# A two-layer kernel of scans, attention and experts: the first side input is loaded alone, its products move to VectorE and PSUM, and the V projections stand right behind the scores

## The chip, the cores and the metric

The kernel runs on one core of a Trainium2 chip. The metric is the device time of one execution in microseconds, which is to be small. Its engines each run their own instruction stream in order and meet at semaphores: TensorE (PE in the profile), VectorE (DVE), ScalarE (ACT), GpSimd (POOL) and SyncE (SP, whose queue issues nearly all transfers here).

## The reference

Inputs are x and a side input f, both 4 x 256 x 256 (batch B, positions T, channels C). Three parts follow one another:

```python
# cond: two decaying sums over the positions, forward and backward, per channel
ek, ekv = exp(min(f, 30)), exp(min(f, 30)) * f
a_t = a_{t-1} * decay + ekv_t          # and b_t with ek_t, in both directions
euk = exp(min(u + f, 30))
y = sigmoid(x) * (nf + nb - ekv + euk * f) / max(df + db - ek + euk, 1e-8) * (0.8 + 0.2 * tf)
# attention over y: 16 heads of 128, causal, softmax
x = x + W_O @ softmax(mask(K(y) Q(y)) / sqrt(128)) V(y)
# a second cond with its own w, u on the new x gives y2; 8 experts, the best 2 weigh in
x = x + sum_e gates[e] * (y2 @ expert_w[e] + expert_b[e])
```

## The kernel before, in words

All products are float32 in three passes: each operand is held as a high part (`_hi`, rounded by ScalarE from PSUM) and a low part (`_lo`, the rest, subtracted by VectorE or GpSimd), and `three` (L847) issues high x high, high x low and low x high. A result in PSUM thus becomes an operand in two steps, a ScalarE copy and then a VectorE subtraction: `qk_high`/`qk_low`, `v_high`/`v_low`, `pT_high`/`pT_low`, `z_high`/`z_low`. Weights get the same split by `refill`, on ScalarE (`w_hi`, L356) and then on GpSimd (`w_lo`, L266).

The attention is 16 blocks (four batches by four groups of four heads) of four units each, one head of one batch to a unit, so 64 units; u is the unit, i = u // 4 its block and h = u % 4. Every engine has a loop `for u in range(UNITS)`, written by hand so that the loops mesh. In unit u TensorE does `scores(u)`, `project_qk(u + 2)`, `values(u - 2)`, `turn(u - 1)` (the transposes of the probabilities), and then in the units with h = 0 or 1 one half of the V projection, `project_v(i, h)`, in those with h = 2 or 3 one half of `output` of the block before. VectorE starts a unit with `v_low` of the V half of the unit before, then `maxima(u)`, `reciprocals(u)`, `qk_low(u + 2)`, `z_low(u - 2)`, `pT_low(u - 1)`. ScalarE does `exps(u)`, `qk_high(u + 2)`, `z_high(u - 2)`, `pT_high(u - 1)`, and `v_high` last. GpSimd multiplies the probabilities by the reciprocals (`shares`, L298) after its other work of the unit. `values(4 i)` stands in unit 4 i + 2 and needs both V halves of block i as high and low parts (`v_ready`).

The conds of the next batches and of the second layer are cut into pieces, which tables (`DVE_PLACES`, `ACT_PLACES`, `POOL_PLACES`) put into the units: "M" behind the maxima or exponentials, "E" at the end of the unit. Eight conds in all; the first, of batch 0, is written out ahead of the loops, since nothing can start without its y. It works by channel half c: `min`, exponentials, forward scans into `f_xd` and `f_xn`, scaling on ScalarE, backward scans, then two long reciprocals and `first_y(c)`. While it runs, TensorE does `WARM` pairs of products whose result nobody reads (L1012).

SP issues the loads in one list: temb, f of batch 0 (`in_f0`), the Q and K weights of group 0, x of batch 0, and so on. Behind the loop come the experts on TensorE (`experts(j)`, 32 of them, with `logits`, `gates_turn` and `base` of the four batches between them) and `add_experts(j)` on VectorE; `acc` goes out in eight stores.

## Time and profile before

| | |
|---|---|
| time, median of 3 runs | 388.52 us (388.48 to 388.64) |
| the profiled execution's own time | 388.69 us |
| its span, first to last instruction | 386.8 us |
| TensorE busy | 357.1 us (92%), 2534 instructions |
| VectorE busy | 315.2 us (81%) |
| ScalarE busy | 219.7 us (57%) |
| GpSimd busy | 210.1 us (54%) |
| mean granted clock of TensorE | 0.994 |

Busy times are sums over the span; ends of matmuls are modelled. The time of a run is 1.9 us above the span in the profiled execution. Times in the rows are microseconds from the span's start; a releaser behind an arrow is what ended the idle time before an instruction.

### The profile page before, as it was taken

To read this page: it belongs to the slowest core of one execution; us is meant where nothing else is said; L and a number is where in the kernel's file an instruction comes from. 1 tells how busy PE (TensorE), PEld (TensorE's weight loads), DVE (VectorE), ACT (ScalarE), POOL (GpSimd) and SP (SyncE) were. 2 spreads that over 40 slices of the span, in tenths; PEclk is the share of its full clock that TensorE was granted. 3 is DMA by queue.
4 is the path that set the end of the run, shared out by engine and by line. 5 is a ranking of instruction groups with operands and counts; after the bars stand their busy time and mean duration, and the time that the engine had idled before them with its cause. 6 is when DMAs were issued, how large, how long until landed. Compare 5 with 4: busy or idle time off the path is not lost.

```text
span 386.8 us, 7608 instructions
## 1 busy us (share of the span) xinstructions
PE 357.1 (92%) x2534; PEld 332.8 (86%) x2534; DVE 315.2 (81%) x883; ACT 219.7 (57%) x616; POOL 210.1 (54%) x231
## 2 busy tenths in 40 slices
PE   0578888999999999999999999999999998999996
PEld 0467878999999899999999999999999987877885
...
DMA packets 4598, 14.14 MB, mean 37 GB/s; under 512 B 840, under 2 KB 1872, under 8 KB 3920
## 3 DMA queue, kind: packets, MB, share of 16 engines
q1 hardware_dynamic: 4416, 13.65, 10.6%
...
q10 hardware_dynamic: 144, 0.00, 0.0%
...
## 4 chain that ended last, share of the span: by engine, by line
PE 81%; DVE 10%; issue 2%; POOL 2%; ACT 2%; DMA 1%; SPq 0%; DVEq 0%; ACTq 0%; POOLq 0%
PE psQK L850 9%; PE psQK L852 9%; PE psQK L851 9%; PE psT L910 5%; PE psZ L850 4%; PE psO L852 4%; PE psO L850 4%; PE psO L851 4%; PE psS L901 4%; PE psS L850 4%; PE psZ L852 4%; PE psZ L851 4%; PE psS L851 4%; PE psS L852 4%; PE psV L850 4%; PE psV L852 3%
## 5 line engine op out<-in xcount | busy, mean ns | idle before, releaser
L472 ACT ACTIVATE prob<-prob,ntop 128x256 f32<-128x256 f32 (+1 forms) x128 | 57.3, 449 | 93.3 <-DVE ntop L690 93.3
L301 POOL TENSOR_SCALAR prob<-prob,rsum 128x128 f32<-128x128 f32 x64 | 38.9, 607 | 104.7 <-DVE rsum L698 104.7
L850 PE MATMUL psQK<-y_hi,w_hi 128*128 128x256 f32 x256 | 73.3, 286 | 1.3 <-DVE y_lo L613 1.1
L852 PE MATMUL psQK<-y_hi,w_lo 128*128 128x256 f32 x256 | 73.0, 285 | 0.0
L851 PE MATMUL psQK<-y_lo,w_hi 128*128 128x256 f32 x256 | 72.9, 285 | 0.0
L302 POOL TENSOR_SCALAR prob<-prob,rsum 128x256 f32<-128x256 f32 x64 | 59.8, 935 | 0.0
L266 POOL TENSOR_TENSOR w_lo<-raw,w_hi 128x512 fp32r<-128x512 f32 x40 | 52.9, 1334 | 6.6 <-ACT w_hi L356 6.4
L850 PEld LDWEIGHTS psQK<-y_hi,w_hi 128*128 128x128 f32 x256 | 49.3, 193 | 2.2 <-DVE y_lo L613 1.3
L852 PEld LDWEIGHTS psQK<-y_hi,w_lo 128*128 128x128 f32 x256 | 49.3, 193 | 0.0
L851 PEld LDWEIGHTS psQK<-y_lo,w_hi 128*128 128x128 f32 x256 | 49.3, 193 | 0.0
L702 DVE TENSOR_TENSOR qk<-psQK,qk 128x512 fp32r<-128x512 f32 x64 | 43.6, 682 | 6.5 <-ACT qk L460 4.8
L850 PE MATMUL psZ<-pT,v_hi 128*128 128x256 f32 x128 | 37.0, 289 | 9.0 <-issue 4.6
L850 PE MATMUL psO<-z_hi,w_hi 128*128 128x256 f32 x128 | 38.6, 302 | 0.0
L460 ACT ACTIVATE qk<-psQK 128x512 fp32r<-128x512 f32 x64 | 36.9, 577 | 0.6 <-PE psQK L852 0.5
L706 DVE TENSOR_TENSOR v_lo<-psV,v_hi 128x512 fp32r<-128x512 f32 x32 | 22.0, 689 | 17.9 <-ACT v_hi L466 17.8
L852 PE MATMUL psZ<-pT,v_lo 128*128 128x256 f32 x128 | 36.1, 282 | 0.0
L851 PE MATMUL psZ<-pT,v_hi 128*128 128x256 f32 x128 | 36.1, 282 | 0.0
L852 PE MATMUL psO<-z_hi,w_lo 128*128 128x256 f32 x128 | 36.1, 282 | 0.0
L851 PE MATMUL psO<-z_lo,w_hi 128*128 128x256 f32 x128 | 36.0, 281 | 0.0
L711 DVE TENSOR_TENSOR pT<-psT,pT 128x384 fp32r<-128x384 f32 x64 | 35.0, 547 | 0.5 <-ACT pT L480 0.5
L850 PEld LDWEIGHTS psZ<-pT,v_hi 128*128 128x128 f32 x128 | 24.3, 190 | 11.2 <-issue 8.9
L910 PE MATMUL psT<-identf,prob 128*128 128x128 f32 x192 | 31.3, 271 | 0.0
...
## 6 DMA issues: line engine op xcount, KB each, us to landing
...
out<-fT SPq DMA_DIRECT2D x8, 128.0 KB, 2.0
...
xT<-in_xT SPq DMA_DIRECT2D x1, 512.0 KB, 10.9
wu<-in_wu ACTq DMA_DIRECT2D x1, 4.0 KB, 1.6
```

The source lines that it names most:

```text
L266: pool.tensor_tensor(w_view(w_lo[:, g % 2], kind, part), w_view(raw, kind, part), w_view(w_hi[:, g % 2], kind, part).bitcast(F32), ALU.sub ...
L301: pool.tensor_scalar(prob[:, k, 0:P], prob[:, k, 0:P], rsum[:, k, 0:1], None, ALU.mult)
L302: pool.tensor_scalar(prob[:, k, P:3 * P], prob[:, k, P:3 * P], rsum[:, k, 1:2], None, ALU.mult).then_inc(shared, 1)
L460: act.activation(qk_hi[:, u % 2], psQK[u % 2][:], ACT.Copy).then_inc(qk_hi_done, 1)
L472: ins = act.activation(prob[:, k, lo:hi], prob[:, k, lo:hi], ACT.Exp, scale=-1.0, bias=ntop[:, k, q:q + 1], accum_out=ssum[:, k, q:q + 1])
L702: dve.tensor_tensor(qk_lo[:, u % 2], psQK[u % 2][:], qk_hi[:, u % 2].bitcast(F32), ALU.subtract).then_inc(qk_ready, 1)
L706: dve.tensor_tensor(v_lo[:, i % 2, t], psV[:], v_hi[:, i % 2, t].bitcast(F32), ALU.subtract).then_inc(v_ready, 1)
L711: dve.tensor_tensor(pT[:, k, 1, P:4 * P], psT[:, 0:3 * P], pT[:, k, 0, P:4 * P].bitcast(F32), ALU.subtract).then_inc(pT_ready, 1)
L850: pe.matmul(out, ah, bh, start=first and k == 0, stop=False)
L851: pe.matmul(out, ah, bl, start=False, stop=False)
L852: ins = pe.matmul(out, al, bh, start=False, stop=last and k == n - 1)
L910: ins = pe.transpose(psT[:, n * P:(n + 1) * P], prob[:, u % 2, c * P:(c + 1) * P], identf[:])
```

## The change

It does five things. SP loads f of batch 0 first and waits until it has landed before it issues the next load; temb goes to ScalarE's queue. In the first cond the products `f_ekv` and `f_eukv` and the clamp of `euk` are no longer GpSimd's but VectorE's, and they stand in PSUM banks (`psQK[1]`, `psT`); ScalarE writes the exponentials once, into PSUM, and `WARM` is 5 instead of 7. V halves are projected right behind the scores of their unit (the first one ahead of all scores), copied right behind the exponentials on ScalarE and subtracted behind the reciprocals of the same unit on VectorE. The shares of units 2 and 3 are ScalarE's. `min` and `exps` of the later conds start a unit earlier, and some weight copies of groups 2 to 4 stand at "M". In the end `gates_copy(0)`, `gates_turn(1)`, `pT_high` of the last unit, `y2_last(3)`, `logits(3)`, `gates_turn(3)` and `base(3)` change their places by one step.

```diff
-DVE_PLACES = {"min": (-2, "E"), "xd": (0, "M"), "xn": (1, "M"), "gd": (2, "M"), "gn": (3, "M"), "den": (4, "M"),
+DVE_PLACES = {"min": (-3, "E"), "xd": (0, "M"), "xn": (1, "M"), "gd": (2, "M"), "gn": (3, "M"), "den": (4, "M"),
...
-ACT_PLACES = {"exps": (-1, "E"), "sxd": (0, "E"), "sxn": (1, "E"), "e1": (2, "E"), "yhi": (7, "E")}
+ACT_PLACES = {"exps": (-2, "E"), "sxd": (0, "E"), "sxn": (1, "E"), "e1": (2, "E"), "yhi": (7, "E")}
...
+SHARES_ACT = (2, 3)
 GATE_STEPS = 14
-WARM = 7
+WARM = 5
...
-    f_ek, f_euk = halves(psQK[0]), halves(psS[0])
+    f_ek, f_ekv, f_euk, f_eukv = (halves(bank) for bank in (psQK[0], psQK[1], psS[0], psT))
     f_xd, f_xn = [psV[:, 0:T], psS[1][:, 0:T]], [psZ[:, 0:T], psO[:, 0:T]]
     t0 = tiles[:, 0]
-    f_e1, f_eukv = t0[:, XD], t0[:, XN]
+    f_e1 = t0[:, XD]
...
-        sp.dma_start(temb[:], ap["temb"]).then_inc(in_temb, 16)
+
         load_f(0, 1, in_f0)
+        sp.wait_ge(in_f0, 16)
         load_qk(0)
...
-
-        pool.wait_ge(f_act, 2)
-        pool.tensor_tensor(t0[:, EKV], t0[:, EK], cols(fT, 0), ALU.mult).then_inc(f_pool, 1)
-        pool.wait_ge(f_act, 4)
-        pool.tensor_scalar(t0[:, EUK], t0[:, EUK], EXP_LIMIT, None, ALU.min).then_inc(f_pool, 1)
-        pool.wait_ge(f_pool, 2)
-        pool.tensor_tensor(f_eukv, t0[:, EUK], cols(fT, 0), ALU.mult).then_inc(f_pool, 1)
...
-            shares(u)
+            if u not in SHARES_ACT:
+                shares(u)
...
+        act.dma_start(temb[:], ap["temb"]).then_inc(in_temb, 16)
         act.dma_start(wu[:], ap["wu"]).then_inc(in_wu, 16)
...
-        act.activation(t0[:, EK], t0[:, EK], ACT.Exp).then_inc(f_act, 1)
-        for c in range(CB):
-            act.activation(t0[:, EUK, c], fT[:, 0, c], ACT.Exp, bias=wu[:, 1, c:c + 1]).then_inc(f_act, 1)
+        for c in range(CB):
+            act.activation(f_euk[:, c], fT[:, 0, c], ACT.Exp, bias=wu[:, 1, c:c + 1]).then_inc(f_act, 1)
...
+        def shares(u):
+            k = u % 2
+            act.wait_ge(recipd, u + 1)
+            act.activation(prob[:, k, 0:P], prob[:, k, 0:P], ACT.Copy, scale=rsum[:, k, 0:1])
+            act.activation(prob[:, k, P:3 * P], prob[:, k, P:3 * P], ACT.Copy, scale=rsum[:, k, 1:2]).then_inc(shared, 1)
...
             for kind, part, u in places:
-                at(u, "E", refill, kind, g, part)
+                at(u, "M" if u % GH < TT and g > 1 else "E", refill, kind, g, part)
...
         at(62, "E", gate_exp, 1)
-        at(63, "M", gates_copy, 0)
+        at(62, "E", gates_copy, 0)
         at(63, "E", gates_copy, 1)
...
         qk_high(0)
         qk_high(1)
+        v_high(0, 0)
         cond(1)["exps"]()
         for u in range(UNITS):
+            i, h = u // GH, u % GH
             exps(u)
+            if h < TT and u:
+                v_high(i, h)
             do(u, "M")
             if u + 2 < UNITS:
                 qk_high(u + 2)
             if 2 <= u:
                 z_high(u - 2)
+            if u in SHARES_ACT:
+                shares(u)
             if 1 <= u:
                 pT_high(u - 1)
             do(u, "E")
-            i, h = u // GH, u % GH
-            if h < TT:
-                v_high(i, h)
         z_high(UNITS - 2)
+        pT_high(UNITS - 1)
         tanh(2)
-        pT_high(UNITS - 1)
...
         for c in range(CB):
             forward(f_xd[c], f_ek[:, c], 0, c, 0).then_inc(f_dve, 1)
+        dve.tensor_tensor(f_ekv, f_ek, cols(fT, 0), ALU.mult).then_inc(f_dve, 1)
         for c in range(CB):
             dve.tensor_scalar(decay[:, 1, c], tdec[:], ew[:, 1, c:c + 1], None, ALU.mult).then_inc(pre_dve, 1)
...
+        dve.wait_ge(f_dve, 4)
+        for c in range(CB):
+            forward(f_xn[c], f_ekv[:, c], 0, c, 0).then_inc(f_dve, 1)
+        for c in range(CB):
+            dve.wait_ge(f_act, 4 + c)
+            backward(t0[:, GD, c], f_xd[c], 0, c, 0).then_inc(f_dve, 1)
+        dve.wait_ge(f_act, 3)
+        dve.scalar_tensor_tensor(f_eukv, f_euk, EXP_LIMIT, cols(fT, 0), ALU.min, ALU.mult).then_inc(f_dve, 1)
+        for c in range(CB):
+            dve.wait_ge(f_act, 6 + c)
+            backward(t0[:, GN, c], f_xn[c], 0, c, 0).then_inc(f_dve, 1)
...
             dve.scalar_tensor_tensor(f_xd[c], f_xd[c], 1e-8, f_e1[:, c], ALU.max, ALU.mult).then_inc(f_dve, 1)
 
         def first_y(c):
             dve.tensor_tensor(f_xn[c], f_eukv[:, c], t0[:, GN, c], ALU.add).then_inc(f_dve, 1)
-            dve.wait_ge(f_dve, 15 + 4 * c)
...
         for u in range(UNITS):
-            if 1 <= u:
-                i, h = (u - 1) // GH, (u - 1) % GH
-                if h < TT:
-                    v_low(i, h)
             maxima(u)
             do(u, "M")
             reciprocals(u)
+            i, h = u // GH, u % GH
+            if h < TT:
+                v_low(i, h)
...
         gate_first(2)
         add_experts(5)
+        y2_last(3)
         gate_last(2)
-        y2_last(3)
         add_experts(6)
         add_experts(7)
+        add_experts(8)
         gate_first(3)
-        add_experts(8)
+        add_experts(9)
         gate_last(3)
-        for j in range(9, 8 * B):
+        for j in range(10, 8 * B):
             add_experts(j)
...
-        pe.wait_ge(f_dve, 6)
+        pe.wait_ge(f_dve, 7)
         for n in range(WARM):
             for c in range(CB):
-                pe.matmul(psQK[1][:, c * T:(c + 1) * T], identf[:], fT[:, 0, c], start=True, stop=True)
+                pe.matmul(psQK[0][:, c * T:(c + 1) * T], identf[:], fT[:, 0, c], start=True, stop=True)
 
         pe.wait_ge(wlo_qk, 2)
-        pe.wait_ge(f_dve, 18)
+        pe.wait_ge(f_dve, 20)
         project_qk_half(0, 0)
         project_qk_half(1, 0)
         y_waits(0)
         project_qk_half(0, 1).then_inc(qk_done, 1)
         project_qk_half(1, 1).then_inc(qk_done, 1)
+        project_v(0, 0)
         for u in range(UNITS):
             i, h = u // GH, u % GH
             scores(u)
+            if h < TT and u:
+                project_v(i, h)
             if u == UNITS - 2:
                 logits(1)
             if u + 2 < UNITS:
@@ -1029,11 +1038,7 @@
                 values(u - 2)
             if u:
                 turn(u - 1)
-            if u == UNITS - 1:
-                gates_turn(1)
-            if h < TT:
-                project_v(i, h)
-            elif i:
+            if h >= TT and i:
                 output(i - 1, h - TT)
             if u == UNITS - 6:
                 logits(0)
@@ -1041,6 +1046,7 @@
                 experts(0)
                 gates_turn(0)
             if u == UNITS - 1:
+                gates_turn(1)
                 base(0)
                 experts(1)
         experts(2)
@@ -1054,7 +1060,7 @@
             output(len(BLOCKS) - 1, c)
         logits(2)
         base(1)
-        late = {7: [(logits, 3)], 9: [(gates_turn, 2)], 10: [(base, 2)], 11: [(gates_turn, 3)], 12: [(base, 3)]}
+        late = {8: [(logits, 3)], 9: [(gates_turn, 2)], 10: [(base, 2)], 12: [(gates_turn, 3)], 13: [(base, 3)]}
         for j in range(6, 8 * B):
```

VectorE in the first cond before, from the first forward scans on (psV and psS are `f_xd`, psZ and psO are `f_xn`; tiles is the SBUF work space):

```order
L569 SCALAR_TENSOR_TENSOR psV<-decay,psQK 128x256
L569 SCALAR_TENSOR_TENSOR psS<-decay,psQK 128x256
L580 TENSOR_SCALAR decay<-tdec,ew 128x4 x2
L583 TENSOR_SCALAR rest<-decay 128x16
L585 SCALAR_TENSOR_TENSOR rest<-decay,rest 128x16
L586 TENSOR_SCALAR tout<-tf 128x4
L588 TENSOR_SCALAR thalf<-tout 128x4
L569 SCALAR_TENSOR_TENSOR psZ<-decay,tiles 128x256
L569 SCALAR_TENSOR_TENSOR psO<-decay,tiles 128x256
```

And the same place in the change:

```order
L573 SCALAR_TENSOR_TENSOR psV<-decay,psQK 128x256
L573 SCALAR_TENSOR_TENSOR psS<-decay,psQK 128x256
L583 TENSOR_TENSOR psQK<-psQK,fT 128x512
L585 TENSOR_SCALAR decay<-tdec,ew 128x4 x2
L588 TENSOR_SCALAR rest<-decay 128x16
L590 SCALAR_TENSOR_TENSOR rest<-decay,rest 128x16
L573 SCALAR_TENSOR_TENSOR psZ<-decay,psQK 128x256
L573 SCALAR_TENSOR_TENSOR psO<-decay,psQK 128x256
```

The product `f_ekv` is a VectorE instruction now (L583), tout and thalf come later, and both scans of `f_xn` read PSUM (psQK) instead of tiles.

VectorE at the end of unit 1 before, from its scans `gd` to the maxima of unit 2:

```order
L572 SCALAR_TENSOR_TENSOR tiles<-decay,tiles 128x256 x2
L698 RECIPROCAL rsum<-ssum 128x2
L702 TENSOR_TENSOR qk<-psQK,qk 128x512
L711 TENSOR_TENSOR pT<-psT,pT 128x384
L572 SCALAR_TENSOR_TENSOR tiles<-decay,tiles 128x256 x2
L706 TENSOR_TENSOR v_lo<-psV,v_hi 128x512
L689 TENSOR_TENSOR first_mask<-psS,negmask 128x128
```

In the change:

```order
L576 SCALAR_TENSOR_TENSOR tiles<-decay,tiles 128x256 x2
L705 RECIPROCAL rsum<-ssum 128x2
L713 TENSOR_TENSOR v_lo<-psV,v_hi 128x512
L709 TENSOR_TENSOR qk<-psQK,qk 128x512
L718 TENSOR_TENSOR pT<-psT,pT 128x384
L576 SCALAR_TENSOR_TENSOR tiles<-decay,tiles 128x256 x2
L696 TENSOR_TENSOR first_mask<-psS,negmask 128x128
```

`v_lo` moved from the place behind the second pair of scans to the place behind the reciprocals, ahead of `qk` and `pT`.

TensorE before, from the transposes of unit 0 on through the second V half to the scores of unit 2:

```order
L910 MATMUL psT<-identf,prob 128x128 x3
L850 MATMUL psV<-w_hi,y_hi 128x512
L851 MATMUL psV<-w_lo,y_hi 128x512
L852 MATMUL psV<-w_hi,y_lo 128x512
L850 MATMUL psV<-w_hi,y_hi 128x512
L851 MATMUL psV<-w_lo,y_hi 128x512
L852 MATMUL psV<-w_hi,y_lo 128x512
L901 MATMUL psS<-qk 128x256 x2
```

In the change, from the scores of unit 1 on to the first product of the next Q and K:

```order
L907 MATMUL psS<-qk 128x256 x2
L856 MATMUL psS<-qk 128x256
L857 MATMUL psS<-qk 128x256
L858 MATMUL psS<-qk 128x256
L856 MATMUL psV<-w_hi,y_hi 128x512
L857 MATMUL psV<-w_lo,y_hi 128x512
L858 MATMUL psV<-w_hi,y_lo 128x512
L856 MATMUL psV<-w_hi,y_hi 128x512
L857 MATMUL psV<-w_lo,y_hi 128x512
L858 MATMUL psV<-w_hi,y_lo 128x512
L856 MATMUL psQK<-y_hi,w_hi 128x256
```

The six products of the V half stand behind the scores (psS) and ahead of twelve products of psQK, which they used to follow, with the transposes.

## Rows read from the trace of the kernel before

**Rows 1.** Waits of TensorE: us in total, times, longest.
```profile
PE psQK L1012 <- DVE tiles L572: 10.3, 1, 10.3
PE psZ L850 <- issue: 4.6, 7, 1.5
PE psZ L850 <- DVE v_lo L706: 3.0, 1, 3.0
...
PE psZ L850 <- DVE pT L711: 1.5, 3, 1.0
PE psV L964 <- ACT tiles L454: 1.1, 1, 1.1
PE psQK L850 <- DVE y_lo L613: 1.1, 1, 1.1
...
PE psV L950 <- DVE y L681: 0.7, 1, 0.7
```

**Rows 2.** The chain that ended last: start, us, what.
```profile
1.32 4.88 DMA fT<-in_fT
...
59.34 1.53 issue
...
97.04 0.48 issue
...
243.67 0.46 issue
...
316.55 0.72 issue
```

**Rows 3.** Timeline of the start, VectorE's, GpSimd's and TensorE's instructions: start, us.
```profile
6.23 0.43 DVE L554 TENSOR_SCALAR tiles<-fT 128x512 f32<-128x512 f32 x1 [6.23 <-DMA fT<-in_fT]
...
8.76 0.58 DVE L580 TENSOR_SCALAR decay<-tdec,ew 128x4 f32<-128x4 f32 x2
...
11.24 1.69 DVE L569 TENSOR_TENSOR_SCAN psO<-decay,tiles 128x256 f32<-128x256 f32 x1
...
12.85 0.66 DVE L572 TENSOR_TENSOR_SCAN tiles<-decay,psV 128x256 f32<-128x256 f32 x1
...
13.65 8.06 PE L1012 MATMUL psQK<-fT,identf 128*128 128x256 f32 x28 [10.35 <-DVE tiles L572]
...
15.21 7.61 POOL L266 TENSOR_TENSOR w_lo<-raw,w_hi 128x512 fp32r<-128x512 f32 x6 [2.84 <-ACT w_hi L356]
15.47 0.42 DVE L600 SCALAR_TENSOR_TENSOR psS<-psS,tiles 128x256 f32<-128x256 f32 x1
...
18.13 1.11 DVE L607 TENSOR_TENSOR psZ<-tiles 128x256 f32<-128x256 f32 x1
...
21.62 1.50 DVE L607 TENSOR_TENSOR psO<-tiles 128x256 f32<-128x256 f32 x1
...
24.57 0.39 PE L850 MATMUL psQK<-y_hi,w_hi 128*128 128x256 f32 x1 [1.06 <-DVE y_lo L613]
```

**Rows 4.** DMA issues of the page: KB each, median us to landing.
```profile
out<-fT SPq DMA_DIRECT2D x8, 128.0 KB, 2.0
```

**Rows 5.** Time to landing of the three loads of xT, by tile.
```profile
DMA to landing us min/median/max: 7.2/9.6/10.9
```

**Rows 6.** Windows: length, busy PE, PEld, DVE, ACT, POOL (instructions), clock, DMA share, GB/s.
```profile
40.00:50.00 10.00, 8.98 (x60) 8.64 (x61) 10.00 (x25) 5.79 (x18) 9.12 (x10) 0.83 0.13 37
50.00:60.00 10.00, 8.65 (x58) 7.53 (x56) 7.64 (x19) 8.42 (x23) 7.69 (x9) 1.00 0.36 121
...
42.00:43.00 1.00, 1.00 (x6) 1.00 (x6) 1.00 (x5) 1.00 (x4) 0.78 (x2) 0.50 0.00 0
```

**Rows 7.** Timeline around 96 us, unit 13 going into 14.
```profile
95.73 0.55 DVE L711 TENSOR_TENSOR pT<-psT,pT 128x384 fp32r<-128x384 f32 x1
...
96.72 0.69 DVE L706 TENSOR_TENSOR v_lo<-psV,v_hi 128x512 fp32r<-128x512 f32 x1 [0.44 <-ACT v_hi L466]
```

**Rows 8.** Waits of VectorE: us in total, times, longest.
```profile
DVE v_lo L706 <- ACT v_hi L466: 17.8, 28, 1.6
```

More of the change, by code:

```diff
@@ L585, in _ @@
         dve.scalar_tensor_tensor(rest[:], decay[:], 1.0, rest[:], ALU.add, ALU.mult).then_inc(pre_dve, 1)
+        dve.wait_ge(f_dve, 4)
[9 more added lines that the diff above has]
+            backward(t0[:, GN, c], f_xn[c], 0, c, 0).then_inc(f_dve, 1)
         dve.tensor_scalar(tout[:], tf[:], 0.2, 0.8, ALU.mult, ALU.add).then_inc(pre_dve, 1)
+        for c in range(CB):
+            dve.wait_ge(f_dve, 7 + c)
+            dve.scalar_tensor_tensor(f_xd[c], f_euk[:, c], EXP_LIMIT, t0[:, GD, c], ALU.min, ALU.add).then_inc(f_dve, 1)
         dve.wait_ge(pre_dve, 10)
         dve.tensor_scalar(thalf[:], tout[:], 0.5, None, ALU.mult).then_inc(pre_dve, 1)
[L589 removed]
+        dve.wait_ge(f_act, 9)
         for c in range(CB):
[L591 to L603 removed]
+            dve.wait_ge(f_dve, 12 + c)
             dve.scalar_tensor_tensor(f_xd[c], f_xd[c], 1e-8, f_e1[:, c], ALU.max, ALU.mult).then_inc(f_dve, 1)
@@ L622, in clamp @@
                 if n == 2:
-                    dve.wait_ge(f_dve, 21)
+                    dve.wait_ge(f_dve, 23)
                 if n > 2:
@@ L861, in y_waits @@
             if b == 0:
-                pe.wait_ge(f_dve, 21)
+                pe.wait_ge(f_dve, 23)
             else:
```

31 lines of the change are left out of this document (8 added, 23 removed).

## The prediction

> **What bounds the kernel now.** I read the waits of TensorE first, since it is busy for 92% of the span. They are few: 10.3 us once, in the start, until VectorE's first backward scan releases the idle warm-up products, and then a handful that add up to about 13 us in the other 360 [rows 1]. So the kernel has two parts that can be shortened: the chain from the first load to the first real product, in which TensorE does nothing useful, and single holes later. The chain that ended last says where those are: an "issue" of 0.48 us at 97.04 comes again with every second block, five times up to the one at 243.67 (0.46), and single ones of 1.53 at 59.34 and 0.72 at 316.55 [rows 2]. Each stands ahead of `values`. The timeline around 96 us shows what "issue" hides: `v_lo` ends at 97.41 and the product starts at 97.52, while the other operand, `pT`, had ended at 96.28 [rows 7]. So the second V half is what comes last.
>
> The timeline of the start gives the other part: VectorE starts at 6.23, when f has landed, and the second half of y reaches TensorE at 24.57 [rows 3]. The windows show a third thing: from 40 to 50 us VectorE is busy for 10.00 of 10 us and TensorE's granted clock has a mean of 0.83; at 42 to 43 it is 0.50, the lower of its two levels (1.2 GHz), after TensorE had waited 3.0 us for `v_lo` [rows 1, 6]. A mean of 0.83 over 10 us is 1.7 us of clock lost.
>
> **The start, -5.2 us.** Three terms.
>
> Landing. The load of f is issued at 1.32 and takes 4.88 us, with a megabyte of weights and more behind it on the same queue [rows 2]. Alone, it is issued at about 0.7, where temb was, and 256 KB should take more than the 2.0 us of a store of 128 KB [rows 4] and at most the 4.88. I take 2.8, nearer to the store, since with nothing beside it the queue holds only this load: VectorE starts at 3.5 instead of 6.2, -2.7 us. Bounds: 2.7 (-3.5) and 5.6 (-0.6). What waits behind: the Q and K weights go out 1.6 us later than before, x of batch 0 at about 4.0. x took 7.2 us, the smallest of its three loads [rows 5]; so it lands at 11.2 and its two ScalarE passes, some 0.6 us each, end near 12.5, just when VectorE comes to the step that needs them. temb on ScalarE's queue delays the tiny loads by half a microsecond, which the wait for f covers.
>
> VectorE's chain up to the first backward scan. From the second pair of decays at 8.76 to that scan at 12.85 it takes 4.09 us [rows 3]. The two forward scans of `f_xn` in it lie beside GpSimd instructions; the second takes 1.69 us, where a scan whose data is in PSUM takes 0.66 [rows 3]. With the GpSimd work gone, scans start every 0.6 us and the small instructions every 0.2: decays 0.35, the two of rest 0.4, two scans 1.2, that is 2.0 us. Added are `f_ekv`, about 0.62 (the same shape from PSUM and SBUF is `v_lo`, 0.69 with 0.07 of overlap [rows 7]), as much for `f_eukv` later, and tout and thalf, 0.3, which only moved. 4.09 against 3.54: -0.55 us. Bounds 0 and -1.2.
>
> The two sums of `first_y`. They take 1.11 and 1.50 us, both operands in SBUF, while GpSimd is in its row of six weight subtractions; the instruction of the same size at 15.47, one operand in PSUM, takes 0.42 beside the same GpSimd work [rows 3]. In the change `f_eukv` stands in PSUM, so both should take 0.4: -0.7 and -1.1, together -1.9 us (bounds 0 and -1.9).
>
> So TensorE's second half of y is ready at 24.57 - 5.15 = 19.4. The first V half, now right behind those products, needs six weight pieces from GpSimd, done at 22.8 before [rows 3]; they start when ScalarE gets to them, at about 12.5 instead of 14.5, so they end near 20.7, and V is asked for at 20.8. Nothing to spare, but no loss.
>
> **Units 0 to 7, -2.6 us.** TensorE's waits here are the 3.0, about 1.2 of the 1.5 for `pT`, the 1.53, and 1.7 of clock [rows 1, 2, 6]. The 3.0 us goes: `v_low` of the second half is done in unit 1. But VectorE has no idle time up to 50 us [rows 6] and the same work to do; one instruction more stands there, `min` a unit earlier (0.5), and the first scores start 0.45 later behind the V half. So `pT_low`, the next in line, is waited for in place of `v_lo`, in two or three pieces of 0.5 to 1.4 us, and unit 4 begins on VectorE some 0.6 us late. The wait of 3.0 in one piece, and with it the drop of the clock, should go. What is won comes behind unit 4: in the window from 50 to 60 VectorE has 2.4 us of idle time [rows 6], in which it waits for `v_hi` on ScalarE, and TensorE then for VectorE. In the new order `v_hi` comes right behind the exponentials, and VectorE can use these 2.4 us. With the 1.53 and the rest of `pT` I take -2.6. Bounds: 0 (all given back) and the sum of what is lost, -7. The shares of units 2 and 3 on ScalarE take two GpSimd instructions of about 1.5 us off the way to the transposes; GpSimd is busy for 9.12 of 10 us there [rows 6], so this mainly lets the weights of group 1 keep up with a V half that is asked for 4 us sooner. I count it at nothing.
>
> **Units 8 to 61, -2.3 us.** Five holes of 0.48 [rows 2]. What the holes wait for now is done a unit ahead. Next in line is `pT_low`. It must be ready when `values` comes; between `turn` and `values` TensorE used to do a V half, the scores and Q and K, now in a unit with h = 1 only the last two, some 2.0 us. In the stretch of rows 7 `pT_lo` stands at 95.73 to 96.28 and would be asked for at 97.04, 0.76 us of slack; in the new order `v_lo` (0.69) comes ahead of it, but no wait for ScalarE does, and VectorE no longer loses the 17.8 us that it waited for `v_hi` in 28 of the 32 V halves, at the head of the unit [rows 8]. So it is in time, and I keep 0.1 us for all of it.
>
> **The end, -2.7 us.** Four holes, each with its own cure: the 0.72 at 316.55 is `v_lo` again [rows 2]; the 1.1 of L964 is `gates_turn(1)`, waiting for `gates_copy(0)`, which ScalarE now does a unit earlier, and one `output` half stands ahead; 0.3 of `pT` is `pT_high` behind `tanh(2)`; the 0.7 of L950 is `logits(3)` waiting for `y2_last(3)`, which is now ahead of `gate_last(2)`, and `logits(3)` comes one expert (1.4 us) later [rows 1]. Sum 2.8; I keep 0.1 for what slips. The last expert, its sums and the store do not change.
>
> **Sum.** -5.15 - 2.6 - 2.3 - 2.7 = -12.75 us on the profiled execution's own 388.69, so 375.9; the median of the runs is 388.52, 0.2 below it. I say 376.0.
>
> **A rule against it.** The warm-up is 20 passes instead of 28 in 8.06 us [rows 3], at the same rates some 6 to 7 us from about 9.2 on, so it ends at 15 to 17, and the first product of y can start at 17.7: 1 to 3 us of idle time where there was 0.1. The one hole of 3.0 us in the trace was followed by the lower level for about 3.4 us [rows 1, 6]. The Trainium skill, "TensorE: Matmul & The Clock Gate", section "Why this matters for your kernels", says that holes of more than about 3 us between bursts bring the half clock back, and the trace agrees with that. By this rule, with the hole at its upper end, the sum would be 377.4 (below) and not 376.0.
>
> **The rivals.**
> - V pieces bring nothing in units 0 to 7, because VectorE is the bound there throughout: 376.0 + 2.6 = 378.6. For it: 10.00 busy of 10. Against: 2.4 idle of the next 10.
> - `pT_low` takes the place of `v_low` in the units with h = 1, so that the five holes stay: 376.0 + 2.3 = 378.3. For it: the slack of 0.76 us and a `v_lo` of 0.69 ahead. Against: VectorE's waits for `v_hi` go.
> - The clock falls behind the shorter warm-up: up to 1.7 us of the first products, of which those that VectorE waits for count, about 1.4: 377.4. This is the case if the idle time comes near the 3.0 us of the hole above; I hold it to stay below.
> - The load of f is no sooner alone, since its 4.88 us is latency: +2.1 at most, 378.1. Against it: 2.0 us for the stores.
> - Slower: the same `pT_low`, but late in the h = 1 unit of each of the 15 blocks behind the first, since ScalarE now does `v_hi` and in places a weight copy ahead of `qk_hi`, `z_hi` and `pT_hi`. Each 0.1 us costs 1.5. At 0.85 us per block it eats all of the 12.75; at 1.0 the time is 391. In rows 7 it would have to come 0.76 + 0.85 us later than now, in a unit of 4.58 us (the holes of rows 2 are 146.6 us and 32 units apart).
>
> **Chances.** Forecast 0.55 (its own range 374.3 to 377.8), VectorE bound 0.18, holes stay 0.10, clock 0.08, load 0.06, slower 0.03. 0.2% (0.8 us) is about what a measurement of this kernel can tell from no change. The other cases all lie below 387, so faster has 0.95; two of them together give 381. I leave 0.02 for the same, where a late `pT_low` happens to cancel the rest. The range reaches down to 373.3 by the bound of units 0 to 7, half used, and up to 380.3, by the landing at half its bound together with the first rival.
>
> **What the profile of the changed kernel would show.** VectorE's first instruction at 3.5 (3.0 to 4.2); the forward scans of `f_xn` at 0.7 us each and the sums of `first_y` at 0.4; the first product of the second half of y at 19.4; TensorE's longest wait behind it below 1.5 us and a granted clock of 1.00 from 30 to 60; no wait ahead of `values` near every second block; in the waits none of L964 and L950. The prediction is wrong if VectorE waits for x behind its scans (x landing after 11.5), if waits of `values` for `pT` come back in every block, or if VectorE's unit 4 begins over 1 us later, counted from the first product, than it did.

## The result

The changed kernel takes 384.2 us, median of 4 runs (383.55 to 384.35), beside 388.5 us for the kernel before (388.3 to 388.64): a ratio of 0.9886, 95% interval 0.9874 to 0.9898. It is faster, by 4.3 us or 1.1%; 376.0 was forecast, with a range of 373.3 to 380.3, so the time lies outside. The profiled execution took 383.55 us, its span is 381.7.

The page of the kernel after, busy time of the engines, then the waits of TensorE (us in total, times, longest), beside [rows 1]:

```profile
PE 354.3 (93%) x2526; PEld 331.3 (87%) x2526; DVE 320.5 (84%) x885; ACT 222.7 (58%) x617; POOL 205.0 (54%) x224
```

```profile
PE psQK L1018 <- DVE tiles L576: 5.7, 1, 5.7
PE psZ L856 <- DVE pT L718: 4.6, 6, 1.4
...
PE psV L856 <- DVE v_lo L713: 3.4, 2, 1.8
PE psQK L856 <- DVE y_lo L620: 2.7, 1, 2.7
PE psQK L856 <- POOL w_lo L269: 2.1, 2, 1.4
PE psV L970 <- DVE logit L737: 0.9, 1, 0.9
```

The wait of the warm-up products for the first backward scan is 4.6 us shorter, the 3.0 for `v_lo` and the five holes "issue" are gone, and so are L964 and L950. What is new or longer: `pT` six times (three before), `y_lo` 2.7 (1.1 before), `v_lo` twice, GpSimd's low weights, and VectorE's copy of the logits.

The timeline of the start, kernel after (start, us), beside [rows 3]:

```profile
3.89 0.43 DVE L558 TENSOR_SCALAR tiles<-fT 128x512 f32<-128x512 f32 x1 [3.89 <-DMA fT<-in_fT]
4.16 0.56 PE L1012 MATMUL psO<-temb,ones 64*128 64x4 f32 x2 [4.16 <-DMA temb<-in_temb]
4.20 0.20 ACT L361 ACTIVATE ew<-wu 128x4 f32<-128x4 f32 x1 [0.98 <-DMA wu<-in_wu]
5.97 0.70 DVE L573 TENSOR_TENSOR_SCAN psV<-decay,psQK 128x256 f32<-128x256 f32 x1
...
9.59 0.66 DVE L576 TENSOR_TENSOR_SCAN tiles<-decay,psV 128x256 f32<-128x256 f32 x1
...
10.40 7.01 PE L1018 MATMUL psQK<-fT,identf 128*128 128x256 f32 x20 [5.69 <-DVE tiles L576]
...
12.34 7.39 POOL L269 TENSOR_TENSOR w_lo<-raw,w_hi 128x512 fp32r<-128x512 f32 x6 [9.53 <-ACT w_hi L353]
12.50 1.14 DVE L602 TENSOR_SCALAR tout<-tf 128x4 f32<-128x4 f32 x1
14.22 0.65 DVE L607 TENSOR_SCALAR thalf<-tout 128x4 f32<-128x4 f32 x1
...
19.89 0.42 DVE L614 TENSOR_TENSOR psO<-psT,tiles 128x256 f32<-128x256 f32 x1
20.12 0.36 PE L856 MATMUL psQK<-y_hi,w_hi 128*128 128x256 f32 x1 [2.71 <-DVE y_lo L620]
21.77 0.39 PE L856 MATMUL psQK<-y_hi,w_hi 128*128 128x256 f32 x1
```

f lands at 3.9, but temb and `wu`, two small loads that used to land before it, land at 4.16 and 4.20. The sum of `first_y` takes 0.42 us, as said. Two instructions on 128 x 4 elements take 1.14 and 0.65 us: the first begins 0.16 us behind GpSimd's first weight subtraction. The second half of y reaches TensorE at 21.77, 2.80 us sooner than before; 5.15 was forecast.

Windows of the kernel after (length, busy PE, PEld, DVE, ACT, POOL, granted clock, DMA share, GB/s), beside [rows 6], and four in unit 62:

```profile
40.00:50.00 10.00, 6.75 (x48) 5.87 (x47) 9.36 (x21) 6.90 (x19) 5.59 (x5) 1.00 0.17 52
50.00:60.00 10.00, 8.13 (x62) 7.51 (x61) 8.94 (x25) 7.90 (x24) 8.48 (x8) 1.00 0.33 107
...
311.00:312.00 1.00, 0.03 (x1) 0.00 (x0) 1.00 (x4) 0.61 (x2) 0.57 (x2) 1.00 0.00 0
312.00:313.00 1.00, 0.87 (x5) 0.87 (x6) 0.97 (x8) 0.35 (x1) 0.97 (x1) 0.67 0.00 0
313.00:314.00 1.00, 1.00 (x7) 1.00 (x6) 0.87 (x9) 0.98 (x5) 0.00 (x0) 0.50 0.00 0
314.00:315.00 1.00, 1.00 (x7) 1.00 (x6) 0.61 (x2) 0.62 (x3) 0.97 (x2) 0.50 0.03 8
```

The drop at 42 us is gone; one at 312.4 to 315.6 is there instead, and its place is unit 62. The timeline there:

```profile
309.99 0.69 DVE L713 TENSOR_TENSOR v_lo<-psV,v_hi 128x512 fp32r<-128x512 f32 x1 [0.32 <-ACT v_hi L461]
310.60 0.68 DVE L709 TENSOR_TENSOR qk<-psQK,qk 128x512 fp32r<-128x512 f32 x1
311.20 0.41 DVE L724 TENSOR_TENSOR z_lo<-psZ,z_hi 128x256 fp32r<-128x256 f32 x1
311.53 0.55 DVE L718 TENSOR_TENSOR pT<-psT,pT 128x384 fp32r<-128x384 f32 x1
...
312.13 0.42 PE L856 MATMUL psZ<-pT,v_hi 128*128 128x256 f32 x1 [1.10 <-DVE pT L718]
```

Units 62 and 63 have no Q and K left to do. The second V half of the last block used to stand between `turn(60)` and `values(60)`; moved ahead, it leaves only the scores and `logits(1)` there, and TensorE is through with them 1.10 us before `pT_low(60)`.

To place gains and losses I read from TensorE's timeline the first matmul of `scores(u)` (us), in before, after and the experiments:

| kernel | u = 0 | 8 | 56 | 61 | 63 | span |
|---|---|---|---|---|---|---|
| before | 27.04 | 67.94 | 287.17 | 310.51 | 321.33 | 386.8 |
| after | 24.70 | 65.72 | 281.78 | 304.96 | 317.76 | 381.7 |
| e1 `tout` early | 23.33 | 64.35 | 280.51 | 303.71 | 315.01 | 379.0 |
| e2 `experts(0)` first | 24.71 | 65.73 | 281.89 | 305.09 | 315.57 | 379.5 |
| e3 old V order in units 0 to 7 | 23.93 | 65.19 | 281.25 | 304.43 | 317.24 | 381.2 |
| e4 f not alone | 28.93 | 71.14 | 287.28 | 310.48 | 323.29 | 387.2 |
| e5 after, again | 25.69 | 67.88 | 284.16 | 307.38 | 318.66 | 382.6 |
| e6 short reciprocals | 24.44 | 62.76 | 278.92 | 302.13 | 313.41 | 377.4 |
| e7 old V order everywhere | 24.93 | 67.47 | 284.79 | 308.13 | 318.96 | 382.9 |
| e11 `min` late | 25.67 | 66.44 | 282.72 | 305.94 | 318.75 | 382.7 |
| e9 combined | 23.36 | 65.53 | 281.76 | 304.98 | 315.48 | 378.3 |
| e13 combined, `min` in unit 3 | 23.36 | 62.95 | 279.01 | 302.19 | 312.70 | 375.5 |

So the 5.1 us of the span come as: second half of y -2.80; from there to unit 8 +0.58 (-2.6 forecast); units 8 to 61 -3.33 (-2.3); the rest +0.45 (-2.7).

### The profile page after: what moved, and what is told of

Its sections match the earlier page's. It is cut to its first block, busy times and chain, and to the rows that moved or that the text cites. A ratio compares the mean times of both kernels' runs of the same rounds, so it can differ in the third digit from the quotient of the medians.

```text
span 381.7 us, 7587 instructions
## 1 busy us (share of the span) xinstructions
PE 354.3 (93%) x2526; PEld 331.3 (87%) x2526; DVE 320.5 (84%) x885; ACT 222.7 (58%) x617; POOL 205.0 (54%) x224
## 3 DMA queue, kind: packets, MB, share of 16 engines
HBM read 12.60 MB, written 1.05 MB: 36 GB/s over the span
## 4 chain that ended last, share of the span: by engine, by line
PE 77%; DVE 17%; ACT 3%; issue 2%; DMA 1%; DVEq 0%; ACTq 0%
PE psQK L856 8%; PE psQK L858 8%; PE psQK L857 8%; PE psT L916 5%; PE psO L856 4%; PE psO L857 4%; PE psO L858 4%; PE psZ L856 4%; PE psZ L857 4%; PE psZ L858 3%; PE psS L856 3%; PE psS L858 3%; PE psS L907 3%; PE psS L857 3%; PE psV L856 3%; PE psV L857 3%
## 5 line engine op out<-in xcount | busy, mean ns | idle before, releaser
L304 POOL TENSOR_SCALAR prob<-prob,rsum 128x128 f32<-128x128 f32 x62 | 37.5, 605 | 94.8 <-DVE rsum L705 94.7
L305 POOL TENSOR_SCALAR prob<-prob,rsum 128x256 f32<-128x256 f32 x62 | 57.5, 927 | 0.0
L481 ACT ACTIVATE pT<-psT 128x384 fp32r<-128x384 f32 x64 | 31.4, 490 | 0.3 <-PE psT L916 0.3
L696 DVE TENSOR_TENSOR first_mask<-psS,negmask 128x128 f32<-128x128 f32 x64 | 18.0, 282 | 14.0 <-PE psS L858 13.8
```

The source lines that it names most:

```text
L304: pool.tensor_scalar(prob[:, k, 0:P], prob[:, k, 0:P], rsum[:, k, 0:1], None, ALU.mult)
L305: pool.tensor_scalar(prob[:, k, P:3 * P], prob[:, k, P:3 * P], rsum[:, k, 1:2], None, ALU.mult).then_inc(shared, 1)
L481: act.activation(pT[:, u % 2, 0, P:4 * P], psT[:, 0:3 * P], ACT.Copy).then_inc(pT_hi_done, 1)
```

## The experiments

In the changed kernels the executions of one kernel differ in time and in mean granted clock, so the clock stands beside the time where it matters. A hole is a stretch in which TensorE is idle, a drop one in which its granted clock is 0.50. Unless said otherwise the edit is on the changed kernel; times at the first scores and at a unit are from one profiled execution each.

### The start

**e1, `tout` and `thalf` early.**

```diff
+        dve.tensor_scalar(tout[:], tf[:], 0.2, 0.8, ALU.mult, ALU.add).then_inc(pre_dve, 1)
+        dve.wait_ge(pre_dve, 10)
+        dve.tensor_scalar(thalf[:], tout[:], 0.5, None, ALU.mult).then_inc(pre_dve, 1)
         dve.wait_ge(f_dve, 4)
         for c in range(CB):
             forward(f_xn[c], f_ekv[:, c], 0, c, 0).then_inc(f_dve, 1)
...
-        dve.tensor_scalar(tout[:], tf[:], 0.2, 0.8, ALU.mult, ALU.add).then_inc(pre_dve, 1)
...
-        dve.wait_ge(pre_dve, 10)
-        dve.tensor_scalar(thalf[:], tout[:], 0.5, None, ALU.mult).then_inc(pre_dve, 1)
```

> The changed kernel (384.2) with one move: `tout` and `thalf` go back right behind `rest`, ahead of the scans of `f_xn`. Behind the scans they took 1.14 and 0.65 us, since GpSimd's first weight subtraction had begun at 12.34. Theory 1 (tiny VectorE instructions are held up by GpSimd's instruction, and they stand on the path to y): each takes about 0.16 again, VectorE reaches the reciprocals 1.2 to 1.5 us sooner, the second half of y reaches TensorE near 20.4 instead of 21.8, and what of it survives units 0 to 7 shows at the end: 382.7 to 384. Theory 2 (the sums and scans beside GpSimd take up the freed time, or x or `f_e1` comes last): no change, second half of y at 21.5 or later. If VectorE is the bound of units 0 to 7 and the start is worth its full size, 1.3 us come through to the end.

Measured 381.49 us (0.9834, 0.9806 to 0.9863); three of six executions at a clock of 1.00 took 380.68 to 380.93. The timeline of e1:

```profile
8.42 0.16 DVE L591 TENSOR_SCALAR tout<-tf 128x4 f32<-128x4 f32 x1
8.62 0.17 DVE L593 TENSOR_SCALAR thalf<-tout 128x4 f32<-128x4 f32 x1
```

Theory 1: they take 0.16 and 0.17 us, and every unit from 0 to 61 begins 1.25 to 1.37 us sooner. So a gain in the start comes through units 0 to 7 in full: they take the same time, whenever they begin. The profile also has the 1.10 us wait in unit 62, and no drop behind it.

**e4, f not alone** (`sp.wait_ge(in_f0, 16)` left out).

> The changed kernel without the wait of the load queue for f: the weights of Q and K and x go out right behind f. Theory 1 (f lands sooner because nothing shares the DMA engines with it): f lands near 5.1 instead of 3.9, the small loads on ScalarE's queue later than 4.2 too, the whole start 0.8 to 1.5 us later, time 385 to 385.7. Theory 2 (f lands sooner only because it is issued 0.6 us sooner): f lands near 3.9 as now, x sooner, no change in the time. Theory 3 (the small loads set the first scan, not f): first scan later by what temb is later.

Measured 387.57 us (0.9966, 0.9954 to 0.9979), at a clock of 1.00 386.49. The timeline of e4:

```profile
5.92 0.43 DVE L557 TENSOR_SCALAR tiles<-fT 128x512 f32<-128x512 f32 x1 [5.92 <-DMA fT<-in_fT]
6.20 0.56 PE L1011 MATMUL psO<-temb,ones 64*128 64x4 f32 x2 [6.20 <-DMA temb<-in_temb]
...
9.00 0.21 ACT L360 ACTIVATE ew<-wu 128x4 f32<-128x4 f32 x1 [5.78 <-DMA wu<-in_wu]
9.54 0.17 DVE L559 TENSOR_SCALAR tf<-tf 128x4 f32<-128x4 f32 x1 [3.19 <-ACT tf L364]
```

f is issued at 0.72 in both and lands 2.0 us later here, so f gains from having no loads behind it, and not from its time of issue. And theory 3 is right as well: `wu`, issued at 1.31 on ScalarE's queue, lands at 9.00 instead of 4.20, and the first scan waits for it. The wait of the load queue is worth 4.2 us at the first scores, more than all of its gain for f.

**e10, temb first** on the load queue, ahead of f; wu alone on ScalarE's.

> The changed kernel with temb issued on the load queue ahead of f, as before the change, and only wu on ScalarE's queue. Theory 1 (the small loads were late because they share the DMA engines with f and are issued at the same time): temb lands at 2.8 to 3.2 instead of 4.16, f is issued 0.4 to 0.6 later and lands near 4.4; the first forward scan starts 1.4 us behind `min` instead of 2.1, that is near 5.8 to 5.9 instead of 5.97: no gain in the time (within 0.3 us at equal clock). Theory 2 (latency alone): the same, with wu as late as temb was. Theory 3 (f is delayed by the full 0.6 and temb still lands at 4): first scan 6.5, time +0.5.

Measured 383.95 us (0.9879, 0.9865 to 0.9893), all at 0.981 to 0.987. temb lands at 2.75, f at 4.58, the first scan starts at 5.93 instead of 5.97: theory 1. So 0.7 us of what f won was lost to the small loads behind it, and putting them first only shifts that loss to f.

### Units 0 to 7

**e6, short reciprocals.**

```diff
-                dve.reciprocal(t[:, GD, c], t[:, XD, c]).then_inc(c_dve[k], 1)
+                m = 8 if n == 1 else T
+                dve.reciprocal(t[:, GD, c, 0:m], t[:, XD, c, 0:m]).then_inc(c_dve[k], 1)
```

> The changed kernel with the two reciprocals of the first stage of batch 1 (they lie in units 2 and 3) cut from 256 columns to 8: it leaves out part of y of batch 1, for the time alone. That takes about 1.7 us of work from VectorE in units 2 and 3 and changes no wait and nothing on the other engines. Theory 1 (VectorE is the bound of units 0 to 7): unit 8 begins 1.2 to 1.7 us sooner, and the time falls by as much at equal clock. Theory 2 (GpSimd's weight subtractions for group 1 are the bound there, since TensorE waits 2.7 us for them): no change or under 0.4 us. Half of each: 0.6 to 1.0.

Measured 379.44 us (0.977, 0.9757 to 0.9783). A reciprocal of 256 columns in the timeline of after and what stands there in e6:

```profile
41.54 1.74 DVE L670 RECIPROCAL tiles<-tiles 128x256 f32<-128x256 f32 x1
```

```profile
41.28 0.19 DVE L671 RECIPROCAL tiles<-tiles 128x8 f32<-128x8 f32 x1
```

I had put the two together at 1.7 us; each takes 1.74, so about 3.1 us of work went. Unit 8 begins 2.96 us sooner, 2.70 counted from the first scores. Nearly nine tenths of the time taken from VectorE comes out at once: it is the bound where the reciprocals stand, in units 2 and 3. GpSimd, whose low weights TensorE waits for, had the same work. VectorE is not full in all of the stretch: in the changed kernel it is busy for 36.6 of the first 40 us from the first scores on.

**e3, old V order in units 0 to 7** (the V pieces of the first two blocks where they stood, on three engines).

> The changed kernel with the V pieces of units 0 to 7 (blocks 0 and 1) in the order of the kernel before on all three engines: V half behind the transposes, `v_high` last in the unit, `v_low` first in the next. Units 8 to 63 stay as changed. Theory 1 (VectorE is the bound of units 0 to 7, so the order of V there is worth nothing): same time within 0.4 us, though single waits move, and a wait of 2 to 3 us with a drop of the clock may come back. Theory 2 (the new order costs there, by a V half asked for before GpSimd has its weights): faster by 0.5 to 1.5. Theory 3 (it gave what was forecast, but something else took it): slower by 1.5 to 2.6.

Measured 383.13 us (0.9878, 0.9859 to 0.9897). The first scores are 0.77 us sooner, unit 8 by 0.53; the 3.0 us for `v_lo` is back, with a clock of 0.50 to 0.58 from 36 to 43 us behind it. Of the 0.77, 0.30 is there before the V half, since the first product of y starts at 19.82 instead of 20.12. Theory 1: the order of V gives nothing here, even with a drop on the side of the old order. What this drop costs is not shown, since no run has this order, otherwise as changed, without one.

**e11, `min` late** (`min` and the exponentials back at -2 and -1, for all stages).

> The changed kernel with `min` and the exponentials of each stage back in the place of the kernel before (two units and one unit ahead of the stage). Theory 1 (the earlier `min` and exponentials took part in the 3.2 us won in units 8 to 61, since with the V order of before only three of the five holes came back): units 8 to 56 take 0.7 to 2 us longer than changed, in holes in the units of the first scans. Theory 2 (it is the V order alone that cures the holes): no change in units 8 to 56 within 0.2 us. In units 0 to 7, where VectorE is the bound, `min` a unit later (it took 1.15 us at 43.3, held up by GpSimd's instruction) gives 0 to 0.6.

Measured 383.39 us (0.9854, 0.984 to 0.9869). Its profile has drops at the same places as e5's up to unit 8, and unit 8 begins 1.44 us sooner than there. Units 8 to 56 take 216.28 us against 216.06: theory 2, 0.2 apart.

**e12, no shares on ScalarE.**

> The changed kernel with the shares of units 2 and 3 on GpSimd, as before the change. The forecast counted their move at nothing. Theory 1 (VectorE is the bound of units 0 to 7, and GpSimd has slack enough): the same within 0.3 us at equal clock. Theory 2 (GpSimd's weight subtractions are late for Q and K, 2.1 us of waits in two pieces): those waits grow and unit 8 begins 0.5 to 2 us later. Theory 3 (less waiting of VectorE's small instructions and scans on GpSimd if it is elsewhere): either sign, up to 0.5.

Measured 384.02 us (0.9885, 0.9866 to 0.9906), 382.59 to 385.33 at clocks of 0.99 to 0.976. That spread covers what was asked, so it is inconclusive by itself; e14 below asks again.

### Units 8 to 61

**e7, all V pieces in the old order,** start and end as changed.

> The changed kernel with all V pieces in the order of the kernel before, on all three engines, in all 64 units; the new start and the new end stay. Theory 1 (the V order gives 3.3 us in units 8 to 61 and nothing in 0 to 7, but costs the 1.1 us wait in unit 62 and the drop behind it): units 8 to 61 3.0 to 3.5 us longer than changed, unit 62 back to 6.3 us from 8.4, time 384.2 + 3.3 - 0.5 - 2.0 = 385 to 386. Theory 2 (units 8 to 61 gained from something else, such as the earlier `min` and exponentials): within 1 us of 382.5. By the forecast for units 8 to 61 (five holes) it would be 2.3 us longer there.

Measured 384.21 us (0.9874, 0.986 to 0.9889). Units 8 to 56 take 217.32 us; 216.06 changed, 219.23 before. So of the 3.2 us there the old order gives back only 1.3; three holes return, not five, of 0.26 to 0.30 us each and in other units (30, 38 and 46). With e11: without the new V order 1.9 is won, without the early `min` 2.95, with both 3.2. Either is much of it, which no part of my sum had foreseen. No run takes back the weight copies at "M", which stand in both, so their share is not separated. The end is as theory 1 said: from u = 61 to 63 it takes 10.83 us, as before (10.82), not 12.80.

### The clock and the end

**e5, the changed kernel again,** and **e8, 28 warm-up passes** (`WARM = 7`).

> The changed kernel unchanged, to see how its executions differ. So far 383.55 at a mean granted clock of 0.994, 384.15 to 384.35 at 0.986 to 0.987; the two experiments of unit 62 and of `tout` had executions at 1.00 that were 1.2 to 4 us faster than their own at 0.98 to 0.99. Theory 1 (each execution loses the clock, or doesn't, at a few places behind short idle times of TensorE): times fall on steps by clock, up to about 2 us apart, and an execution without a drop would take 381.9 to 382.3. Theory 2 (the drop at 312 us is a fixed part of the program's course): all executions within 383.4 to 384.5, none at 1.00.

> The changed kernel with 7 instead of 5 turns of warm-up (28 passes): they end near 20.2 instead of 17.4, and the idle 2.7 us ahead of the first product of y go. Theory 1 (the idle time in the start is one of the places where an execution can lose the clock): executions at 0.986 to 0.987 become rarer, median 0.5 to 1 us lower. Theory 2 (it costs nothing at 2.7 us, and drops come from the wait in unit 62): no change, 383.5 to 384.3. Theory 3 (the warm-up ends too late): first product up to 0.3 us later and the time 0.3 longer.

Measured: e5 384.0 us (0.9883, 0.9862 to 0.9903), from 382.94 at 0.991 over 384.5 at 0.987 to 385.91 at 0.981; e8 383.32 us (0.9869, 0.9849 to 0.989), 381.96 at 1.00, 383.1 to 383.4 at 0.991 to 0.994, 384.66 and 384.95. The waits of the profiled e5, and some of its windows:

```profile
PE psQK L856 <- DVE y_lo L620: 3.1, 1, 3.1
```

```profile
20.00:21.00 1.00, 1.00 (x10) 1.00 (x10) 0.52 (x2) 0.41 (x2) 0.00 (x0) 0.98 0.40 102
21.00:22.00 1.00, 1.00 (x7) 1.00 (x6) 0.76 (x2) 1.00 (x2) 0.43 (x1) 0.50 0.87 209
...
33.00:34.00 1.00, 1.00 (x7) 1.00 (x6) 0.91 (x4) 1.00 (x6) 0.92 (x2) 0.50 0.00 0
45.00:46.00 1.00, 1.00 (x6) 1.00 (x5) 1.00 (x2) 0.00 (x0) 1.00 (x2) 0.50 0.00 0
```

In this execution the lower level comes three times in the start and in units 1 to 5, and not in unit 62. It costs 0.99 us up to the first scores and 2.16 up to unit 8. So the two drops between cost 1.2 us, though VectorE is busy for most of that stretch: the first scores to unit 8 take 42.20 us, 41.02 in the first profile; and e9 with two such drops takes 42.17, e1 with none 41.02. In e5 all of it is lost by unit 4, which begins 19.31 us behind the first scores instead of 18.04.

The drop in the start goes with the hole ahead of y. The same 20 passes of the warm-up take 7.01 us in the first profile and less in this one, so the hole behind them is 2.71 us there and 3.08 here:

```profile
10.32 6.44 PE L1018 MATMUL psQK<-fT,identf 128*128 128x256 f32 x20 [5.69 <-DVE tiles L576]
```

In the profiles of e5, e7, e11 and e12 that hole is 3.06 to 3.52 us, and the level falls at 20 to 21 us each time. At 1.8 to 2.9 us it does not in the first profile, e1, e2, e3, e4 and e6, and does once, at 2.77 in e10. In the first profile it came in unit 62 alone, where u = 61 to 63 took 12.80 us against 11.30 in e1, whose program is the same there: 1.50. So 383.55 - 1.50 = 382.05 would be an execution with no drop, e8's 381.96 is one, and the median of 384.2 holds some 2.1 us of clock. Theory 1 of e5. e8 leaves the start hole at 0.6 us and its profile has no drop at 21, but two later; e9, e13, e14 and e15, with 24 passes and holes under 0.9 us, have none at 21 either. That speaks for the longer warm-up as a cure of the drop in the start. In the time it is not shown: the median is 0.7 lower than e5's, and the spreads overlap.

**e2, `experts(0)` ahead of `values(60)`.**

```diff
             if u == UNITS - 2:
                 logits(1)
+                experts(0)
...
             if u == UNITS - 2:
-                experts(0)
                 gates_turn(0)
```

> The changed kernel with `experts(0)` ahead of `values(60)` in unit 62, instead of behind `turn(61)`: 1.4 us of products in a hole of 1.10 us, in which TensorE waited for `pT_low(60)`. Theory 1 (the V half that moved ahead was the cover of that wait, and the granted clock fell to 0.50 because of the hole): no wait there, clock 1.00 from 310 to 320, unit 62 back to 6.3 us from 8.4, time -1.1 - 0.8 to -1.7, that is 381.5 to 382.4. Theory 2 (the clock falls at this place for another reason, such as the small products of logits): wait gone, clock still 0.50 for 3 us, time -1.0 or less (383.2). Theory 3 (VectorE is late anyway and the wait comes back behind `experts(0)`): no change.

Measured 382.16 us (0.985, 0.9828 to 0.9871): 381.2 and 381.34 at 1.00, three others up to 383.92. The wait is gone, u = 61 to 63 takes 10.48 us: 0.82 less than e1 without a drop, 2.3 less than the first profile. Theory 1 for the place; the other drops, in the start, stay.

**e9, combined:** e1, e2, 24 warm-up passes, and `gates_turn(2)` and `base(2)` one expert later.

```diff
-        late = {8: [(logits, 3)], 9: [(gates_turn, 2)], 10: [(base, 2)], 12: [(gates_turn, 3)], 13: [(base, 3)]}
+        late = {8: [(logits, 3)], 10: [(gates_turn, 2)], 11: [(base, 2)], 12: [(gates_turn, 3)], 13: [(base, 3)]}
```

> The changed kernel with four small moves: `tout` and `thalf` early, `experts(0)` ahead of `values(60)`, 24 warm-up passes instead of 20 (TensorE waited 2.0 us ahead of y with the early `tout`), and in the end `gates_turn(2)` and `base(2)` one expert later (for the 0.92 us wait for the logits). By the parts: -1.3, -1.1, 0, and at most -0.9, from 382.0 for an execution of the changed kernel without a drop of the clock: 378.7 to 379.8 at clock 1.00. Theory 1 (drops come behind idle times): with the idle 2.7 in the start now 0.6 and the wait in unit 62 gone, most executions stand at 1.00 and the median is 379 to 380.5. Theory 2 (drops come by chance wherever units 0 to 7 wait, too): executions at 0.98 to 0.99 as often as before, median 381 to 382. If the last wait is only moved, 0.9 more.

Measured 379.0 us (0.9757, 0.9744 to 0.9769): 378.83 at 1.00, 379.92 and 380.14 at 0.991. The parts add up, and TensorE has no hole over 0.31 us behind unit 8; from u = 63 to the end it takes 62.82 us, 63.94 after: the 0.92 is gone. Its profiled execution still has 0.50 at 29 and at 42 us.

**e13, e9 with `min` and exponentials of stage 2 in units 3 and 4; e14, also the shares on GpSimd; e15, also the old V order in units 0 to 7.**

```diff
-                at(u if n == 1 else COND_START[n] + u, place, pieces[name])
+                at(u if n == 1 else COND_START[n] + u + (n == 2 and name == "min"), place, pieces[name])
```

> The combined kernel (379.0 median, 378.83 at clock 1.00) with `min` and the exponentials of stage 2 alone one unit later, in units 3 and 4, as before the change; all later stages keep the earlier place. Theory 1 (the earlier `min` falls into VectorE's full stretch and is held up there by GpSimd's instruction; with all stages moved back, unit 8 began 1.4 us sooner at the same drops of the clock): 0.5 to 1.4 us faster at equal clock, 377.4 to 378.3, all of it in units 0 to 7. Theory 2 (the work is only moved inside the stretch that VectorE bounds): within 0.3.

> As the kernel with `min` in unit 3, and the shares of units 2 and 3 back on GpSimd. With them alone moved back on the changed kernel, unit 8 began 0.4 us sooner than in an execution with fewer drops of the clock. Theory 1 (the shares on ScalarE delay ScalarE's other work, on which VectorE waits, more than they relieve GpSimd): 0.3 to 0.8 faster than with `min` in unit 3 alone. Theory 2 (counted at nothing, as in the forecast): within 0.2. Theory 3 (GpSimd late with weights): slower by 0.3 or more.

> As the kernel before it, and the V pieces of units 0 to 7 in the old order: the start of the scores is then 0.46 sooner, the wait of 3 us for `v_lo` in unit 3 comes back. Theory 1 (VectorE alone sets units 0 to 7, a V half ahead of the first scores costs 0.46 of it, and drops of the clock cost nothing where VectorE is the bound): 0.3 to 0.6 faster at unit 8, and a drop behind the 3 us wait. Theory 2 (drops of the clock cost there too): slower by 0.5 to 1. Theory 3: within 0.2.

Measured: e13 377.62 us (0.9728, 0.9713 to 0.9743), 377.34 at 1.00, the fastest kernel here; e14 378.36 (0.9734, 0.9721 to 0.9747), 377.67 at 1.00; e15 378.25 (0.9732, 0.9719 to 0.9746), 378.14 to 378.56 at 0.991 to 0.998. `min` in the timeline of after, and in e13:

```profile
43.20 1.24 DVE L638 TENSOR_SCALAR tiles<-fT 128x512 f32<-128x512 f32 x1
```

```profile
46.06 0.42 DVE L638 TENSOR_SCALAR tiles<-fT 128x512 f32<-128x512 f32 x1
```

Unit 8 begins 1.40 us sooner than in e1, neither profile with a drop up to there: theory 1. This is for `min` and the exponentials together; 0.82 of it is the length of `min` itself. Theory 1 of e14 is refuted: the shares on ScalarE do not cost time. They give 0.05 to 0.33 us at a clock of 1.00, one execution against three, which can hardly be told from nothing; but the waits of e14 have the sign of its theory 3, GpSimd late with weights, where e13's longest wait of this kind for V is 0.6:

```profile
PE psV L856 <- POOL w_lo L269: 2.5, 1, 2.5
```

e15 is within 0.5 of e14 with the sign open.

Here is the clock's riddle at its shortest. TensorE's timeline in e9, then in e13; up to 40 us the two run the same program:

```profile
27.97 0.61 PE L856 MATMUL psV<-w_hi,y_hi 128*128 128x512 f32 x1 [1.82 <-DVE v_lo L713]
```

```profile
27.98 0.47 PE L856 MATMUL psV<-w_hi,y_hi 128*128 128x512 f32 x1 [1.82 <-DVE v_lo L713]
```

The same wait of 1.82 us at the same time: e9 goes on at 0.50 up to 31.5, e13 at 1.00.

## Why the prediction was wrong

- **Landing (-2.7).** f alone took 3.2 us and not 2.8, so VectorE starts at 3.9, -2.3. What failed besides is the sentence that temb's half microsecond on ScalarE's queue "the wait for f covers". temb and wu, issued together with f, land behind it; from `min` to the first scan it takes 2.08 us, where it took 1.35 (6.23 to 7.58). e10 shows the cause. The term came to -1.6.
- **The chain to the first backward scan (-0.55).** Its instructions were sized rightly, `tout` and `thalf` excepted: "0.3, which only moved". They moved beside GpSimd's subtractions and took 1.79; counted from start to start of the rows, the term came to about +0.55. The row for this stood in [rows 3]: two tiny decays in 0.58 us beside GpSimd; after, with GpSimd idle there, the same two take 0.35. The Trainium skill ("SBUF — State Buffer", section "Who interferes with whom") says that `tensor_scalar` can take both port pairs and then blocks fully against GpSimd; the trace agrees, with 1.14 us beside GpSimd and 0.16 in e1, and so for instructions of four columns. e1 measures 1.37 us for it.
- **The sums of `first_y` (-1.9).** Right: 0.40 and 0.42 us.
- **Units 0 to 7 (-2.6).** The step that failed is "what is won comes behind unit 4": the 2.4 us of idle time from 50 to 60 were to be used. That was the rival "VectorE is the bound there throughout", which I gave 0.18. e6 shows the bound for units 2 and 3, e3 that the V order is worth nothing there; "throughout" is too much, since VectorE still has 3.4 idle of 40 us. Worse, `min`, put at 0.5 us, fell into VectorE's full stretch beside GpSimd, took 1.24 and, with its exponentials, cost 1.4 (e13). The first V half added 0.46 ahead of the scores.
- **"1.7 us of clock lost" before.** Nothing was to be had: the executions of before at 1.00 and at 0.991 to 0.996 take 388.5 to 388.8 alike. That drop lay where VectorE is busy for 10.00 of 10 us; the two of e5 and of e9, the first of which lies earlier in the same stretch, did cost.
- **Units 8 to 61 (-2.3).** Right in mechanism for three of the five, too small: -3.33. A hole of 0.48 in the chain costs 0.71, read from the start of one scores to the next (5.22 us, 4.51 without), 3.5 for five; two of 0.24 us stayed in after, ahead of `values` in units 14 and 22, at 0.5 each, and eight units without a hole got 0.13 shorter (35.84 us, 35.97 before).
- **The end (-2.7).** I took the 0.72 for gone. The V half that moved was the cover of `pT_low(60)`, the step that I had checked for the middle of the kernel ("now in a unit with h = 1 only the last two, some 2.0 us") and not for unit 62, where there are no Q and K. And `gate_first(3)` came later, so that `gates_turn(2)`, which waits for its copy of the logits, has a new wait of 0.92 in place of the 0.7 (e9 cures it by moving `gates_turn(2)`). One more `add_experts` stands ahead of it, and `y2_last(3)` ahead of `gate_last(2)`, which now runs beside GpSimd's `y_lo`, started at 339.51. One of its four instructions on 128 x 8 elements took 1.36 us, the others 0.28 or 0.29, as all four did before:

```profile
339.48 1.36 DVE L760 TENSOR_SCALAR gsec<-iota,bestf,gw 128x8 f32<-128x8 f32 x1
```

  That is `tout` again; no run separates the two. The end came to -1.05 without the clock.
- **The clock (rival, 0.08).** It costs the median about 2.1 us. I looked at one hole, the warm-up's, and held it to stay below 3.0 us; it was 2.71 in the first profile and over 3 in four others, with a drop each time. The rule that I quoted from the Trainium skill ("TensorE: Matmul & The Clock Gate", "Why this matters for your kernels"), holes over some 3 us, fits those four, and does not tell the rest: the level fell behind 1.10 us in unit 62 and behind 1.82 in e9, and with the same waits it stayed up in e1 and e13; behind 2.97 us in e15 it stayed up too. The measurement decides: shorter holes can do it, and not in each execution.
- **The range.** The bounds that I named for it do not add up to it: half of the way to -7 in units 0 to 7 gives 373.8, and half of the landing's 2.1 with the first rival 379.7, where I wrote 373.3 and 380.3. The result lies outside of either.

The sum: of the 7.6 us between the forecast and the profiled execution, 2.35 lie in the start, 3.2 in units 0 to 7, 1.65 in the end and 1.5 in the clock; units 8 to 61 returned 1.0. What decides whether an execution loses the clock behind one of the shorter holes stays open; for the drop in the start the profiles speak for the length of the hole ahead of y, and the times do not show it.
